# Key-innermost one-hots from 16-bit operands in a graph kernel's sort and permutation, and another order beside its last five node tiles

## The reference

```python
def _L0_gnn_ref(h, relvectors, w_ih, w_hh, b_ih, b_hh, edge_src, edge_dst, edge_rel):
    msg = h[edge_src] + relvectors[edge_rel]
    red = jax.ops.segment_sum(msg, edge_dst, num_segments=h.shape[0])
    return _gru_cell(red, h, w_ih, w_hh, b_ih, b_hh)

def _L1_gnn_ref(x, W, edge_index):
    src, dst = (edge_index and self loops)
    deg = jax.ops.segment_sum(ones, src, num_segments=N)
    vals = rsqrt(deg)[src] * rsqrt(deg)[dst]
    msgs = vals[:, None] * (x @ W.T)[dst]
    return jax.ops.segment_sum(msgs, src, num_segments=N)

x = _layernorm(x + _L0_gnn_ref(x, ..., src, dst, edge_type_16))
x = _layernorm(x + _L1_gnn_ref(x, L1_gnn_W, edge_index))
```

## Time and profile before

| | us |
|---|---|
| median of 3 runs | 2148.17 (2143.56 to 2148.48) |
| the profiled execution | 2143.22 |
| its span in the profile | 2141.5 |

### The profile page before, as it was taken

One profiled execution on the slowest core, in us unless ns is written; L12 is line 12 of the kernel. 1 busy time (PEld: TensorE's weight loads), 2 busy tenths in 40 slices (PEclk: granted clock), 3 DMA queues, 4 the chain that ended last, 5 costly groups with the idle time before them and its releaser, 6 DMA issues. The chain is left out here.

```text
span 2141.5 us, 41955 instructions
## 1 busy us (share of the span) xinstructions
PE 1912.4 (89%) x9416; PEld 1473.0 (69%) x9416; DVE 1716.4 (80%) x3029; ACT 915.9 (43%) x3073; POOL 1542.2 (72%) x1633
## 2 busy tenths in 40 slices
PE   3889989799999998999997899999989999877997
PEld 2667767467777776777775688776767776756886
DVE  6499989899999968888886889788767887544676
ACT  2100000136666634444343998487735877000123
POOL 6667777777777777677666777777777777777771
PEclk8999999899999999999999999999999999999999
DMA  6345555444444455666664333333333333333334
GB/s 169 99 147 168 179 167 172 128 134 144 143 145 145 143 155 165 189 192 187 193 184 126 103 106 106 101 106 105 106 107 107 107 106 106 106 107 106 107 106 139
DMA packets 125298, 289.62 MB, mean 135 GB/s; under 512 B 30214, under 2 KB 60374, under 8 KB 124908
## 3 DMA queue, kind: packets, MB, share of 16 engines
q0 software_dynamic: 77504, 211.67, 34.4%
q10 hardware_dynamic: 37120, 64.87, 8.8%
q1 hardware_dynamic: 10444, 10.38, 1.6%
HBM read 254.81 MB, written 38.40 MB: 137 GB/s over the span
## 5 line engine op out<-in xcount | busy, mean ns | idle before, releaser
L1815 PE MATMUL ps<-rows,onehot 128*128 x5632 | 1335.0, 391 | 110.4 <-SPq L474 51.1
L1815 PEld LDWEIGHTS ps<-rows,onehot 128*128 128x128 f32 x5632 | 1063.9, 193 | 316.0 <-issue 149.4
L616 POOL DMA_INDIRECT rows<-in_x_dram,tidx x815 | 780.5, 958 | 286.9 <-issue 236.1
L637 POOL DMA_INDIRECT rows<-gdram,tidx x784 | 742.0, 946 | 260.4 <-issue 240.6
L951 DVE TENSOR_TENSOR sums<-sums,ps 128x256 f32 x390 | 162.8, 417 | 239.4 <-PE ps L1815 219.6
L910 DVE SCALAR_TENSOR_TENSOR onehot<-tkey,node_p,ps 128x512 f32<-128x512 f32 x400 | 295.8, 739 | 14.4 <-issue 10.2
L968 DVE TENSOR_TENSOR sums<-ps,sums 128x800 f16<-128x800 f32 (+1 forms) x156 | 215.4, 1413 | 1.2 <-issue 1.2
L858 DVE SCALAR_TENSOR_TENSOR onehot<-tkey,node_p,ps 128x1024 f32<-128x1024 f32 x152 | 193.1, 1270 | 2.5 <-DVE steps_i L838 1.0
L1569 ACT ACTIVATE wT<-wT,a 128x208 f16<-128x208 f16 x312 | 116.1, 454 | 123.1 <-DVE wT L852 123.1
L1514 ACT COPY sums<-ps 128x256 f32<-128x256 f32 x49 | 18.2, 372 | 341.6 <-PE ps L1871 341.6
L1530 ACT ACTIVATE sums<-sums 128x50 f32<-128x50 f32 x416 | 94.9, 230 | 106.4 <-DVE sums L1032 106.4
(11 more groups left out here) (313 smaller groups left out, 2037.6 us busy)
## 6 DMA issues: line engine op xcount, KB each, us to landing
xpd<-sums ACTq DMA_DIRECT2D x48, 384.0 KB, 3.4
sums<-xpd ACTq DMA_DIRECT2D x48, 384.0 KB
rows<-in_x_dram,tidx POOLq DMA_INDIRECT x815, 2.9
rows<-gdram,tidx POOLq DMA_INDIRECT x784, 2.7
xt<-in_x_dram ACTq DMA_DIRECT2D x80, 128.0 KB, 2.4
gdram<-in_x_dram ACTq DMA_DIRECT2D x5, 1250.0 KB
gdram<-sums ACTq DMA_DIRECT2D x48, 128.0 KB
out_dram<-sums SPq DMA_DIRECT2D x5, 896.0 KB
```

The lines of the kernel that those rows point to most:

```text
L616: pool.indirect_dma_start(rows[0:z, slot * RS:slot * RS + D], None, x[:, :], bass.IndirectOffsetOnAxis(ap=tidx[0:z, column:column + 1], ax ...
L637: pool.indirect_dma_start(rows[:, slot * D:slot * D + D], None, gdram[:, :], bass.IndirectOffsetOnAxis(ap=tidx[:, column:column + 1], axis ...
L1815: prod = M.matmul(ps[:, h, 0:width], onehot[:, u % U, k, :], rows[:, bass.ds(at + k * stride, width)], start=(k == 0), stop=(k == q - 1))
```

## The change

1. A table `numbers` (208 x 8, 16-bit, in SBUF) repeats every number eight times. ACT fills it once at the start, before it clears `sums0`.
2. `one_hot` and `round_hots` read this table and 16-bit keys. The key is now the innermost index of the result: `oh_lo` is 128 x 16 instead of 16 x 128, `oh_hi` 50 x 16, and the permutation's sets are 128 x 8 and 208 x 8. `prepare_second` makes the 16-bit keys, ordered by round, with three more copies. `seen` and `prod` take the same new order.
3. What reads one key's one-hot now reads with a step: 16 elements of 2 bytes for both operands of L1844; 8 elements of 2 bytes for ACT's inputs in L1538 and L1569, for one operand of PE's L1961 and the weights of L1969; 16 elements of 4 bytes for L1035 and L1530.
4. `soon_c` and `soon_f` move into another buffer.
5. Beside the last five node tiles, PE does both walk steps before `counts_over` and `inputs`, and ACT does the first `put_g` right behind `tanh_of` and `open_gates` behind `sums_over`.

```diff
+        numbers = sb("numbers", [P, G, PB], F16)
-        oh_lo = early(2, SUB, P, dt=F16)
-        oh_hi = early(2, SUB, B, dt=F16)
+        oh_lo = early(2, P, SUB, dt=F16)
+        oh_hi = early(2, B, SUB, dt=F16)
...
-                step(V.scalar_tensor_tensor(lo1, hi1, -float(P), lo1, ALU.mult, ALU.add))
+                step(V.scalar_tensor_tensor(mask, hi1, -float(P), lo1, ALU.mult, ALU.add))
...
+                note(V.tensor_copy(by_round(lo16), by_column(mask)))
+                step(V.tensor_copy(by_round(moved), by_column(hi1)))
+                note(V.tensor_copy(hi16, moved))
...
             def one_hot(out_ap, keys, count, width):
                 return V.tensor_tensor(
-                    out_ap, ps[:, 6, 0:width].rearrange("p (a v) -> p a v", a=1).to_broadcast([P, count, width]),
-                    keys.rearrange("p (k a) -> p k a", a=1).to_broadcast([P, count, width]), ALU.is_equal)
+                    out_ap, numbers[:, 0:width, :],
+                    keys.rearrange("p (a k) -> p a k", a=1).to_broadcast([P, width, count]), ALU.is_equal)
...
             def round_hots(out_ap, keys, r, width):
-                each = SUB // CH
-                now = keys.rearrange("p (g w) -> p g w", g=CH)[:, :, bass.ds(r * each, each)]
+                twice = SUB // PB
                 return V.tensor_tensor(
-                    out_ap.rearrange("p (g i) v -> p g i v", g=CH),
-                    ps[:, 6, 0:width].rearrange("p (g i v) -> p g i v", g=1, i=1).to_broadcast([P, CH, each, width]),
-                    now.rearrange("p g (i v) -> p g i v", v=1).to_broadcast([P, CH, each, width]), ALU.is_equal)
+                    out_ap.rearrange("p v (t k) -> p v t k", t=twice),
+                    numbers[:, 0:width, :].rearrange("p v (t k) -> p v t k", t=1).to_broadcast([P, width, twice, PB]),
+                    keys[:, r * SUB:(r + 1) * SUB].rearrange("p (v t k) -> p v t k", v=1, t=twice
+                                                             ).to_broadcast([P, width, twice, PB]), ALU.is_equal)
...
-                    prod[:, 0, :].rearrange("p (g i b) -> p g i b", g=CH // 2, b=B), axis=AX_X))
+                    prod.rearrange("p a w -> p (a w)").rearrange("p (b g i) -> p g i b", g=CH, b=B)[:, 0:CH // 2], axis=AX_X))
...
+            act.wait_ge(s_const, 1)
+            A.copy(numbers[:, :, :], iota[:, 0:G].rearrange("p (v k) -> p v k", k=1).to_broadcast([P, G, PB])).then_inc(s_sums0, 1)
...
-                    A.activation(bufs[2 + w][:, k, :], bufs[0][:, k, :], ACT.Identity,
+                    A.activation(bufs[2 + w][:, k, :], bufs[0][:, :, k], ACT.Identity,
...
-                        A.activation(slot[2][k][:, w * G:(w + 1) * G], slot[1][:, k, :], ACT.Identity,
+                        A.activation(slot[2][k][:, w * G:(w + 1) * G], slot[1][:, :, k], ACT.Identity,
...
-                    last = M.matmul(ps[:, 4 + a, z:z + B], oh_lo[:, h, q, :], oh_hi[:, h, q, :],
+                    last = M.matmul(ps[:, 4 + a, z:z + B], oh_lo[:, h, :, q], oh_hi[:, h, :, q],
...
-                        last = M.matmul(ps[:, 7, w * G:(w + 1) * G], slot[2 + w][:, k, :], slot[1][:, k, :],
+                        last = M.matmul(ps[:, 7, w * G:(w + 1) * G], slot[2 + w][:, k, :], slot[1][:, :, k],
...
-                    last = M.matmul(ps[:, 7, 0:2 * G], slot[0][:, k, :], slot[2][k], start=False, stop=False)
+                    last = M.matmul(ps[:, 7, 0:2 * G], slot[0][:, :, k], slot[2][k], start=False, stop=False)
...
+                if j == 0:
+                    pe.wait_ge(s_acc[0], J + 2)
+                walk_step(1, D, j + 1, (j + 1) % U, 1)
                 if t < NT - 2:
                     counts_over(t + 2)
                 if t < NT - 1:
                     inputs(t + 1)
-                if j == 0:
-                    pe.wait_ge(s_acc[0], J + 2)
-                walk_step(1, D, j + 1, (j + 1) % U, 1)
```

More of the change, by code:

```diff
@@ L232, in perm_set @@
         def perm_set(hots, buckets):
-            return hots(PB, P, dt=F16), buckets(PB, G, dt=F16), hots(PB, P, dt=F16), hots(PB, P, dt=F16)
+            return hots(P, PB, dt=F16), buckets(G, PB, dt=F16), hots(PB, P, dt=F16), hots(PB, P, dt=F16)
+        hi16, lo16 = hi1.bitcast(F16)[:, 0:C], lo1.bitcast(F16)[:, 0:C]
+        moved = lo1.bitcast(F16)[:, C:2 * C]
         free = again(begin_b, begin_b + SUB * P)
@@ L336, in build @@
         spare = [words16(onehot[:, u, H1:H, :].rearrange("p k v -> p (k v)")[:, 0:2 * G], 2, 2 * G) for u in range(U)]
-        perm1 = [(words16(flat[:, 0:places], PB, P), words16(flat[:, places:places + columns], PB, G),
+        perm1 = [(words16(flat[:, 0:places], P, PB), words16(flat[:, places:places + columns], G, PB),
                   [joint[:, k, :] for k in range(PB)]),
-                 (late(PB, P, dt=F16), words16(bias[:, 0:columns], PB, G), [spare[k // 2][:, k % 2, :] for k in range(PB)])]
+                 (late(P, PB, dt=F16), words16(bias[:, 0:columns], G, PB), [spare[k // 2][:, k % 2, :] for k in range(PB)])]
         scratch1 = late(2 * G)
@@ L714, in prepare_second, with by_round, by_column @@
                 floor_of(hi1, lo1, P)
-                step(V.scalar_tensor_tensor(lo1, hi1, -float(P), lo1, ALU.mult, ALU.add))
+                step(V.scalar_tensor_tensor(mask, hi1, -float(P), lo1, ALU.mult, ALU.add))
+                def by_round(a):
+                    return a.rearrange("p (r g i) -> p g r i", g=CH, i=SUB // CH)
+                def by_column(a):
+                    return a.rearrange("p (g r i) -> p g r i", g=CH, i=SUB // CH)
+                note(V.tensor_copy(by_round(lo16), by_column(mask)))
+                step(V.tensor_copy(by_round(moved), by_column(hi1)))
+                note(V.tensor_copy(hi16, moved))
                 floor_of(a32[:, :], scan, 8)
                 step(V.scalar_tensor_tensor(pos, a32[:, :], -8.0, scan, ALU.mult, ALU.add))
-                step(V.scalar_tensor_tensor(b32[:, :], pos, float(P), lo1, ALU.mult, ALU.add))
+                step(V.scalar_tensor_tensor(b32[:, :], pos, float(P), mask, ALU.mult, ALU.add))
             def own_loops():
@@ L1017, in first_places @@
                 floor_of(share, share, P)
-                V.tensor_copy(seen.rearrange("p a w -> p (a w)"), share).then_inc(s_seen, 1)
+                V.tensor_copy(seen.rearrange("p a w -> p (a w)").rearrange("p (b k) -> p k b", k=SUB),
+                              share.rearrange("p (k b) -> p k b", k=SUB)).then_inc(s_seen, 1)
             def buckets_of(r, h):
-                round_hots(oh_hi[:, h], hi1, r, B).then_inc(s_o2, 1)
+                round_hots(oh_hi[:, h], hi16, r, B).then_inc(s_o2, 1)
             def places(r, h):
-                hots = oh_hi[:, h].rearrange("p (a s) b -> p a (s b)", a=2)
+                hots = oh_hi[:, h].rearrange("p (a b) s -> p a (b s)", a=2)
                 dve.wait_ge(s_run, r + 1)
@@ L1334, in _ @@
             plan(W0)
[L1335 removed]
+            dve.wait_ge(s_sums0, 2)
             walk(0, FIRST)
@@ L1527, in half_places @@
                 act.wait_ge(s_prod, r + 1)
+                placed = prod.rearrange("p a w -> p (a w)").rearrange("p (b s) -> p s b", s=SUB)
                 for q in range(SUB // 2):
                     column = (CH // 2 + q // (SUB // CH)) * G + q % (SUB // CH)
-                    A.activation(dump[:, q, :], prod[:, 1, q * B:(q + 1) * B], ACT.Identity,
+                    A.activation(dump[:, q, :], placed[:, SUB // 2 + q, :], ACT.Identity,
                                  accum_out=pos[:, bass.ds(r * (SUB // CH) + column, 1)]).then_inc(s_part, 1)
@@ L1669, in _ @@
                 tanh_of(t, t % 2)
+                put_g(first, first % U, group_of(first), P)
                 if t < NT - 2:
                     counts_over(t + 2)
-                if t < NT - 1:
-                    open_gates(t + 1, (t + 1) % 2)
-                put_g(first, first % U, group_of(first), P)
-                for d in more:
-                    put_g(d, d % U, group_of(d), P)
-                if t < NT - 2:
-                    sums_over(t + 2)
                 centre(t, t % U)
@@ L1681, in _ @@
                     load_node(t + 3)
+                if t < NT - 2:
+                    sums_over(t + 2)
+                if t < NT - 1:
+                    open_gates(t + 1, (t + 1) % 2)
+                for d in more:
+                    put_g(d, d % U, group_of(d), P)
             for d in LAST_NODES[NT]:
@@ L1848, in hots_of @@
             def hots_of(h, a):
-                return oh_hi[:, h, a * (SUB // 2):(a + 1) * (SUB // 2), :].rearrange("p s b -> p (s b)")
+                return oh_hi[:, h, a * (B // 2):(a + 1) * (B // 2), :].rearrange("p b s -> p (b s)")
             def place_round(r, h):
```

9 lines of the change are left out of this document (4 added, 5 removed).

## The result

The changed kernel takes 2457.5 us (median of 4 runs, 2456.7 to 2458.7), the kernel before 2145.9 beside it: a ratio of 1.145, 95% interval 1.144 to 1.147. That is slower, as forecast, but by 312 us where 89 were forecast, and outside the range. The profiled execution has a span of 2456.1 us, 315 more than the one before.

The account below looks back on a forecast made before the run. POOL's gathers were taken as the bound. To the profiled 2143.2 us came +25 (first layer), +48 (chunk 1's indices), +21 (second layer's hold) and -5 (last five tiles): +89, 2232, or 2237 as median; range 2175 to 2310.

Parts of the forecast that it names:

- The bound and DVE: POOL's gathers, one every 1.25 us, are the bound; DVE's one-hots fall to 1.22, 0.57, 0.69 and 1.02 us.
- The hold: DVE instructions with both operands in SBUF delay POOL's gathers: 38 us in the first layer, 31 in the second.
- +25 for the first layer: First layer's net loss from DVE's hold and the extra copies, against 32 us of room, between +8 and +40.
- +21 for the second: Second layer's 31 us of hold, without the 10 beside chunk 0, where POOL waits anyhow.
- 38 and 2.4: First layer: 38 us of DVE's hold on gathers, and 2.4 us for `prepare_second`'s three added copies.
- rival 1: Hold as forecast, but ACT's stepped reads are free: 2186 to 2196 us; chance 20%.
- PE's moving operand in the first layer's batches: Stepped read at L1961 in 26 batches beside placing, taken as zero.
- Counting: PE's stepped operands in L1844 might add 0.4 us a round, within the 1.47 that DVE gives back.
- Rival 2: As forecast, and PE's stepped weights bind in counting: +1.6 us a round, +62 us, 2299 us; chance 12%.
- ACT's copies: Stepped reads add 0.15 us a copy, 2.4 a batch: +48 us before chunk 1, none in chunks 2 and 3.
- The last five tiles: New order removes PE's waits for ACT's sums copy: -5 us, between 0 and -10.
- The sign: Whole kernel: slower with chance 0.83, same 0.04, faster 0.13.

Follow-up runs that it names:

- e11: Kernel before plus the last five tiles' new order; only counting's and placing's one-hots from SBUF, two keys innermost: 2162.3 us, ratio 1.008.
- e12: Kernel before plus the last five tiles' new order; only the first layer's batch one-hots from SBUF, two keys innermost: 2158.4 us, ratio 1.006.
- e3: Changed kernel with only two keys innermost in all one-hots, so readers step 4 bytes: 2189.4 us, ratio 1.021 to the kernel before.
- e1: Changed kernel with the permutation's one-hots in both layers as before the change: 2173.9 us, ratio 1.013 to the kernel before.
- e9: Kernel before plus the last five tiles' new order; only the first layer's n one-hot from SBUF, eight keys innermost: 2290.3 us, ratio 1.068.
- e6: Changed kernel with long steps only for PE's weights (oh_lo 16 keys, second layer's m 8), other one-hots two keys innermost: 2191.5 us.
- e7: Changed kernel with long steps only for oh_hi (16 keys) and the n one-hots (8), other one-hots two keys: 2444.9 us, ratio 1.140.
- e4: Kernel before with only the new order beside the last five node tiles: 2143.7 us, ratio 0.9987.
- e8: Changed kernel with one key after the other, table and keys 16-bit in SBUF, all readers contiguous: 2348.6 us, ratio 1.095 to the kernel before.

## Why the prediction was wrong, point by point

- **The bound and DVE.** Right: POOL's 1.25 us a gather, and DVE's four durations. That DVE's gain is worth nothing while POOL isn't waiting for it was in the sum, and e11 and e12 show it.
- **The hold.** Right in mechanism and size. The sum's +25 for the first layer and +21 for the second are measured in e3 as +24 and +21 (the gathers' lateness at the end of the first layer, and what the second added to it). The parts are right too: e3's gathers take 40 us longer in the first layer, for 38 and 2.4, POOL's waits there fall by 15, and chunks 0, 1 and 2 have 10, 7 and 9 for 10 each. e12's batches, with 19 for 10, are the exception. Held gathers end 0.81 to 0.83 behind DVE's instruction, as the earlier trace rows had it. (The row at 144.16 was misread: its 3.18 us are one `oh_lo` of 2.28 and one `oh_hi` of 0.98, not two `oh_lo`. What it shows, an unheld gather under them, stands.) Without the readers' step the forecast would be rival 1's 2186 to 2196, and e3 took 2189. In the changed kernel itself the hold in the first layer is not paid on top, because PE is later still there and waits for no gather (e1).
- **PE's moving operand in the first layer's batches: the step that failed worst.** "Taken as zero, for rows there show PE idle beside DVE." It costs 4.44 us a batch, 115 us of PE, and some 46 more by the clock, 161 together, of which 147 are paid (e9). The earlier trace rows has PE busy for 95% of that stretch, 17 us idle in 350, so not even half a microsecond a step had room; and the bound from the earlier trace rows, 1.3 to 1.9 times, was put on ACT but not on this. It was a wrong bound as well: 208 columns take 89 ns in place, 184 with a step of 8 bytes and 366 with 16, four times as long.
- **Counting.** The forecast hid +0.4 us a round. It is +1.18 (0.57 to 1.75), 52 x 1.18 = 61 us of PE. About half of that went into time in which PE had waited for DVE or stood between two instructions; 31 us are left at step 48. With the hold under them they make +30 (e1). Rival 2 had such a cost, with +1.6 and 62 us, but put it on the weights: alone, these make it 1.13 us a round (e6), the moving operand alone 1.65 (e7).
- **ACT's copies.** The term was right in kind and too small: +0.20 a copy, where +0.15 was taken and 0.17 was thought the end (16 a batch: +3.2 against 2.4). Chunk 1's indices came 71 us late instead of 48. That chunks 2 and 3 would not feel it was a slip in the sum's own numbers: a batch of 8.14 us does not fit three steps of about 7.3. Measured are 9.0 a batch, and PE waits for it inside its walk: +33 for each of chunks 1 and 2. The 29 us by which the indices were early did not help, since PE and with it the ring fell behind first: chunk 2's indices are ready at 1872.5, 16 us before POOL's first gather of that chunk (1888.36).
- **The last five tiles.** Forecast -5, measured -2.5 in e4: the waits that go are followed by ones for DVE.
- **Chances.** The sign was right. Of the 312 us, 268 come from the readers' step (e3), where the forecast had 48, all of them ACT's. The range's upper end, 2310, left out the far end of rival 2; had the unknown price of PE's step been carried with the same 1.9 times on 26 batches, it would have added 26 x 1.4 = 37 us, and the true factor of nearly four was not in any row of before.

The Trainium skill, "SBUF — State Buffer", section "Specifications (TRN2)", says that SBUF has lines of 16 bytes and needs two hits in a line for full bandwidth. ACT and DVE agree with that here. Eight of ACT's copies take 2.96 us at 4 bytes, 3.1 at 8 (two hits in a line) and 4.55 at 16 (one); DVE's reduction takes 0.57 at 8 and 0.87 at 16. PE's moving operand does not agree: it is nearly free at 4 bytes (93 ns for 89), but twice as slow at 8 and four times at 16. The same page, section "Who interferes with whom", has a DVE instruction with two SBUF inputs contend with a GpSimd instruction that reads SBUF; e8 against e4 agrees, with 205 us.

## What to carry to other kernels

A layout that gives the writer its double rate is paid by its readers: count their instructions first, with the price of their step, on the engine that has the least idle time. Key pairs innermost (4 bytes of 16-bit values) keep DVE's double rate and cost the readers next to nothing (a batch of PE 1.65 us for 1.59); 8 or 16 keys do not. Even the pairs lost 43 us here, for the one-hots from SBUF hold POOL, and DVE's gain is worth nothing while POOL doesn't wait for it. And an engine that is busy for 98% is not the bound if the one that is doesn't wait for it: look at who waits, not at who is busy.
